# Weight transposes moved into the first aggregation of a graph network, with in-degrees of two chunks on VectorE

## The reference

```python
def _sage_layer(h, edge_src, edge_dst, deg_inv, W_self, W_neigh, b):
    msg = h[edge_src]
    agg = jax.ops.segment_sum(msg, edge_dst, num_segments=h.shape[0])
    mean = agg * deg_inv[:, None]
    return h @ W_self + mean @ W_neigh + b
# _L0_gnn_ref
deg = segment_sum(ones, edge_dst);  deg_inv = 1.0 / jnp.maximum(deg, 1.0)
h = relu(_sage_layer(x, ..., W_self0, W_neigh0, b0))
out = _sage_layer(h, ..., W_self1, W_neigh1, b1)
# _L1_gnn_ref: h = x @ W.T + b, symmetric normalisation by degree, self loops added
x = _layernorm(x + _L0_gnn_ref(x, ...))
x = _layernorm(x + _L1_gnn_ref(x, ...))
```

## Time and profile before

| | us |
|---|---|
| median of 3 runs | 849.19 |
| lowest and highest run | 848.74 and 851.98 |
| the profiled execution | 849.59 |
| its span | 847.9 |
| PE busy | 830.6 (98%) |
| DVE busy | 461.3 (54%) |
| POOL busy | 459.1 (54%) |
| ACT busy | 177.4 (21%) |
| granted TensorE clock, mean | 0.999 |

### The profile page before, as it was taken

The page is one execution under the profiler, slowest core; times in us unless marked ns, Lnnn a source line. Parts: engine busy times, 40 slices in busy tenths (PEclk is TensorE's granted clock), DMA queues, the critical chain, the costliest instruction groups (busy, mean ns, idle before and its releaser), DMA issues.

```text
span 847.9 us, 11000 instructions
## 1 busy us (share of the span) xinstructions
PE 830.6 (98%) x4295; PEld 707.9 (83%) x4295; DVE 461.3 (54%) x714; ACT 177.4 (21%) x218; POOL 459.1 (54%) x343
## 2 busy tenths in 40 slices
PE   8999999999999999999999999999999999999996
PEld 6888888888897899788888888778889889988885
DVE  6465568200017565897544677775556435455555
ACT  4111132110111113353123112222222122200000
POOL 5028887787777887885888788788620000000000
PEclk9999999999999999999999999999999999999999
DMA  9977965463776425668876668267877649555551
GB/s 332 380 304 267 350 193 168 125 176 75 213 236 180 122 57 133 249 237 286 298 282 222 243 220 284 62 176 214 240 245 255 223 150 295 189 199 199 198 193 46
DMA packets 99480, 180.52 MB, mean 213 GB/s; under 512 B 15474, under 2 KB 75898, under 8 KB 94048
## 3 DMA queue, kind: packets, MB, share of 16 engines
q1 hardware_dynamic: 60144, 124.17, 44.0%
q10 hardware_dynamic: 26896, 40.65, 13.3%
q0 software_dynamic: 12384, 14.95, 7.6%
HBM read 107.08 MB, written 72.43 MB: 212 GB/s over the span
## 4 chain that ended last, share of the span: by engine, by line
PE 61%; POOL 15%; DMA 9%; issue 8%; DVE 5%; SPq 1%; ACT 1%; POOLq 0%; ACTq 0%; DVEq 0%
PE ps L1572 19%; POOL adj_in L643 14%; PE ps L1429 12%; PE ps L1606 10%; PE ps L1589 9%; PE ps L1515 8%; DMA adj_in<-u 4%; DMA first_rows<-in_L_gnn_W_neigh 1%; DMA spare<-in_x 1%; DMA xin<-s0t_scr 1%; PE ps L1413 1%; DVE u L914 1%; PE ps L1380 1%; SPq L514 1%; DVE sacc L1303 0%
## 5 line engine op out<-in xcount | busy, mean ns | idle before, releaser
L643 POOL DMA_INDIRECT adj_out<-loops,idx_out x160 | 245.2, 1533 | 65.4 <-issue 65.4
L643 POOL DMA_INDIRECT adj_in<-mult,idx_in x160 | 198.1, 1238 | 86.8 <-issue 86.8
L1572 PE MATMUL ps<-u 128*128 128x512 f32 x840 | 190.7, 389 | 1.4 <-DVE u L914 1.4
L1572 PEld LDWEIGHTS ps<-u 128*128 128x128 f32 x840 | 157.6, 188 | 34.2 <-issue 1.6
L1484 PE MATMUL ps<-wx 128*128 128x512 f32 (+1 forms) x576 | 109.4, 351 | 1.3 <-ACT outb L761 1.3
L1484 PEld LDWEIGHTS ps<-wx 128*128 128x128 f32 x576 | 93.9, 189 | 16.9 <-ACT outb L761 1.9
L1429 PE MATMUL ps<-u 128*128 128x512 f32 x432 | 98.2, 389 | 0.0
L1515 PE MATMUL ps<-wx,u 128*128 128x256 f32 (+5 forms) x640 | 94.8, 309 | 1.2 <-DVE ht L1191 1.2
L1589 PE MATMUL ps<-u,panel_tiles 128*128 128x512 f32 (+1 forms) x400 | 93.9, 393 | 1.9 <-DVE u L914 1.9
L1429 PEld LDWEIGHTS ps<-u 128*128 128x128 f32 x432 | 81.0, 188 | 16.8
L1515 PEld LDWEIGHTS ps<-wx,u 128*128 128x128 f32 (+1 forms) x640 | 86.6, 191 | 8.2 <-DVE ht L1191 1.6
(11 more groups left out here) (167 smaller groups left out, 779.8 us busy)
## 6 DMA issues: line engine op xcount, KB each, us to landing
left_scr<-u SPq DMA_DIRECT2D x7, 2560.0 KB, 9.5
u<-left_scr SPq DMA_DIRECT2D x7, 2560.0 KB, 9.6
xt_scr<-wx ACTq DMA_DIRECT2D x10, 1024.0 KB, 9.9
u<-xt_scr SPq DMA_DIRECT2D x10, 1024.0 KB, 5.1
wx<-xt_scr SPq DMA_DIRECT2D x16, 512.0 KB, 4.0
adj_in<-u POOLq DMA_DIRECT2D x4, 1600.0 KB, 25.3
adj_out<-u POOLq DMA_DIRECT2D x4, 1600.0 KB, 16.1
wx<-adj_in SPq DMA_DIRECT2D x5, 1280.0 KB, 7.1
```

The lines of the kernel that those rows point to most:

```text
L643: pool.indirect_dma_start(table, bass.IndirectOffsetOnAxis(ap=index[0:EP, j:j + 1], axis=0), counts[0:EP, j:j + 1], None, bounds_check=CEL ...
L1572: ins = nc.tensor.matmul(ps[:, product_bank(g, i, p), :], left_op[n % 2][:, p, k, left, :], right_op[n % 2][:, k, right, :], start=(not on ...
```

## The change

- The 8 row transposes of `w_gcn` leave `mean1` and go into `mean0`, behind blocks 3, 8, 12, 14, 17, 20, 23 and 26 (`TURN_BEHIND`). There is now one slot to load into (`turn_in`) and one to copy to (`turn_out`). SP loads rows 1 to 7 ahead of its steps for blocks 7, 12, 16, 18, 21, 24 and 27 (`TURN_LOADS`); ACT copies and stores behind the ReLU of blocks 0, 5, 8, 10, 13, 16, 19 and 23 (`TURN_COPIES`).
- For chunks 0 and 1 the 10 degree matmuls are replaced: DVE sums the panel over its 10 rows of tiles (`tensor_reduce` into `sacc`), copies the sum to `colsum`, and PE makes one matmul with ones (`degrees`), behind block 0 in chunk 0 and behind block 11 (the fourth) in chunk 1. Chunks 2 and 3 keep their 10 matmuls, and now wait for the copy of a turned row, since rows are turned into the same two banks.
- The one-row matmuls for the 1/degree column and DVE's copy of it go. SP stores each chunk's row of 1/degree to memory and loads the column from there once.
- The self parts of blocks 0 to 3 are loaded during `self_turned`. The load of `b1` into `bias` comes after the blocks, because `colsum` lies in the same memory.

```diff
+    TURN_BEHIND = {3: 0, 8: 1, 12: 2, 14: 3, 17: 4, 20: 5, 23: 6, 26: 7}
+    TURN_LOADS = {7: 1, 12: 2, 16: 3, 18: 4, 21: 5, 24: 6, 27: 7}
+    TURN_COPIES = {0: 0, 5: 1, 8: 2, 10: 3, 13: 4, 16: 5, 19: 6, 23: 7}
...
+        turn_in = at("turn_in", [P, D], F32, WX_AT + 4 * (OPS + 3 * PSIZE))
+        turn_out = at("turn_out", [P, D], F32, WX_AT + 4 * (OPS + 3 * PSIZE + D))
...
-        bias = sb("bias", [P, D], F32)
+        bias = at("bias", [P, D], F32, B_AT)
+        colsum = at("colsum", [P, WIDE], F32R, B_AT)
...
+            def fetch_self(m):
+                c, d = H_BLOCKS[m]
+                for i in [S0_BLOCKS.index((b, d)) for b in {0: (0,), 1: (0, 1), 2: (1,), 3: (2,)}[c]]:
+                    sp.wait_ge(s0_stored[i % 4], 16 * (i // 4 + 1))
+                if m >= 4:
+                    sp.wait_ge(h_sum, fetch_free(m))
+                sp.dma_start(fetch_slot(m)[:, 0:CHUNKS[c][1] * T], s0t_scr[d, :, lines(CHUNKS[c])]).then_inc(s0_in[m % 8], 16)
...
+                if i == 20:
+                    sp.wait_ge(xt_turned, NT)
+                    for m in range(4):
+                        fetch_self(m)
...
+            def load_turn(k):
+                if k == 0:
+                    sp.wait_ge(s0_full, 3 * KD)
+                else:
+                    sp.wait_ge(wt_turned, k)
+                sp.dma_start(turn_in[:, :], w_gcn[k * P:(k + 1) * P, :]).then_inc(wt_in, 16)
+
+            load_turn(0)
             sp.wait_ge(m1_full[0], 16)
             load_chunk_1(1)
 
 
-            sp.wait_ge(xt_turned, NT)
             for m, (c, d) in enumerate(H_BLOCKS):
...
+                if m in TURN_LOADS:
+                    load_turn(TURN_LOADS[m])
                 if m >= 4:
-                    sp.wait_ge(h_sum, fetch_free(m))
-                sp.dma_start(fetch_slot(m)[:, 0:CHUNKS[c][1] * T], s0t_scr[d, :, lines(CHUNKS[c])]).then_inc(s0_in[m % 8], 16)
+                    fetch_self(m)
                 if m in (15, 23):
                     load_chunk_1(2 + m // 17)
+                if d == 6:
+                    t0, n = CHUNKS[c]
+                    sp.wait_ge(dinv_row_done, c + 1)
+                    sp.dma_start(dinv_scr[lines(CHUNKS[c])].rearrange("(a j) -> a j", a=1), dinv_row[0:1, c % 2, 0:n * T]
+                                 ).then_inc(dinv_stored[c % 2], 16)
...
+            for s in range(2):
+                sp.wait_ge(dinv_stored[s], 16 * 2)
+            sp.dma_start(dinv[:, :], dinv_scr.rearrange("(t p) -> p t", p=P), allow_slow_non_contiguous=True).then_inc(dinv_in, 16)
+            sp.wait_ge(deg_full, 4)
+            sp.dma_start(bias[:, :], b1.rearrange("(a d) -> a d", a=1).broadcast_to([P, D])).then_inc(bias_full, 16)
...
+            def keep_turned(k):
+                act.wait_ge(wt_turned, k + 1)
+                if k > 0:
+                    act.wait_ge(wt_stored, 16 * k)
+                nc.scalar.activation(turn_out[:, :], pair_bank(3), ACT.Copy).then_inc(wt_copied, 1)
+                act.wait_ge(wt_copied, k + 1)
+                act.dma_start(wt_scr.rearrange("(k p) o -> p k o", p=P)[:, :, k * P:(k + 1) * P],
+                              turn_out.rearrange("p (k o) -> p k o", k=KD)).then_inc(wt_stored, 16)
...
+                if m in TURN_COPIES:
+                    keep_turned(TURN_COPIES[m])
...
-                if 1 <= t <= KD:
-                    k = t - 1
-                    act.wait_ge(wt_turned, k + 1)
-                    nc.scalar.activation(late[:, k % 2, :], pair_bank(3), ACT.Copy).then_inc(wt_copied, 1)
-                    act.wait_ge(wt_copied, k + 1)
-                    act.dma_start(wt_scr.rearrange("(k p) o -> p k o", p=P)[:, :, k * P:(k + 1) * P],
-                                  late[:, k % 2, :].rearrange("p (k o) -> p k o", k=KD)).then_inc(wt_stored[k % 2], 16)
...
                 if d == 0:
+                    if c < 2:
+                        dve.wait_ge(m1_full[c], 16 * n // 2)
+                        nc.vector.tensor_reduce(sacc[:, 0:width].rearrange("p (n j) -> p n j", n=n // 2),
+                                                m1_panels[c][:, :, :, :].bitcast(F32).rearrange("p k n j -> p n j k"), AX_X, ALU.add
+                                                ).then_inc(colsum_done, 1)
+                        dve.wait_ge(colsum_done, 2 * c + 1)
+                        nc.vector.tensor_copy(colsum[:, 0:width], sacc[:, 0:width]).then_inc(colsum_done, 1)
                     dve.wait_ge(deg_full, c + 1)
                     if c >= 2:
-                        dve.wait_ge(dcol_full, c - 1)
+                        dve.wait_ge(dinv_stored[c % 2], 16)
                     nc.vector.tensor_scalar(row, ps[:, 6 + c % 2, 0:width], 1.0, None, ALU.max).then_inc(deg_read, 1)
                     dve.wait_ge(deg_read, c + 1)
                     nc.vector.reciprocal(row, row).then_inc(dinv_row_done, 1)
...
-                if d == 5:
-                    dve.wait_ge(dcol_full, c + 1)
-                    nc.vector.tensor_copy(dinv[:, t0:t0 + n], ps[:, 6 + c % 2, 0:n]).then_inc(dcol_read, 1)
...
+                        dve.wait_ge(wt_stored, 16 * KD)
...
+            dve.wait_ge(dinv_in, 16)
...
-            def turn_weights(c):
-                pe.wait_ge(wt_in[c % 2], 16 * (c // 2 + 1))
-                if c == 0:
-                    pe.wait_ge(*summed(1, 6, 2))
-                else:
-                    pe.wait_ge(wt_copied, c)
+            def turn_weights(row, c):
+                pe.wait_ge(wt_in, 16 * (row + 1))
+                pe.wait_ge(deg_read, c + 1)
+                if row > 0:
+                    pe.wait_ge(wt_copied, row)
                 for k in range(KD):
-                    ins = nc.tensor.transpose(pair_bank(3)[:, k * P:(k + 1) * P], late[:, c % 2, k * P:(k + 1) * P], ident[:, :])
+                    ins = nc.tensor.transpose(pair_bank(3)[:, k * P:(k + 1) * P], turn_in[:, k * P:(k + 1) * P], ident[:, :])
                 ins.then_inc(wt_turned, 1)
...
+            def degrees(c, width, exact):
+                pe.wait_ge(s0_free, s0_bank_free(6 + c))
+                if c == 1:
+                    pe.wait_ge(wt_copied, 2)
+                pe.wait_ge(colsum_done, 2 * c + 2)
+                bank = ps[:, 6 + c % 2, 0:width]
+                if exact:
+                    ins = nc.tensor.matmul(bank, ones_r[:, :].bitcast(F32), sacc[:, 0:width], start=True, stop=True)
+                else:
+                    ins = nc.tensor.matmul(bank, ones_r[:, :], colsum[:, 0:width], start=True, stop=True)
+                ins.then_inc(deg_full, 1)
...
-                    if c < 2:
-                        pe.wait_ge(s0_free, s0_bank_free(6 + c))
-                    else:
-                        pe.wait_ge(dcol_read, c - 1)
-                    for k in range(NT):
-                        ins = nc.tensor.matmul(ps[:, 6 + c % 2, 0:width].rearrange("p (n j) -> p n j", n=n // 2), typed(ones_r[0:rows(k), :], exact),
-                                               typed(panels[0:rows(k), k, :, :], exact), start=(k == 0), stop=(k == NT - 1))
-                    ins.then_inc(deg_full, 1)
+                    if c >= 2:
+                        pe.wait_ge(deg_read, c - 1)
+                        pe.wait_ge(wt_copied, {2: 4, 3: 7}[c])
+                        for k in range(NT):
+                            ins = nc.tensor.matmul(ps[:, 6 + c % 2, 0:width].rearrange("p (n j) -> p n j", n=n // 2),
+                                                   typed(ones_r[0:rows(k), :], exact), typed(panels[0:rows(k), k, :, :], exact),
+                                                   start=(k == 0), stop=(k == NT - 1))
+                        ins.then_inc(deg_full, 1)
                     for d in range(KD):
...
-                        if d == 2:
-                            pe.wait_ge(dinv_row_done, c + 1)
-                            for i in range(n):
-                                ins = nc.tensor.matmul(ps[:, 6 + c % 2, i:i + 1], dinv_row[0:1, c % 2, i * T:(i + 1) * T],
-                                                       ones_nt[0:1, 0:1], start=True, stop=True)
-                            ins.then_inc(dcol_full, 1)
+                        if (c, d) in ((0, 0), (1, 3)):
+                            degrees(c, width, exact)
+                        if m in TURN_BEHIND:
+                            turn_weights(TURN_BEHIND[m], 0 if m == 8 else c)
...
-                        if 1 <= t <= KD:
-                            turn_weights(t - 1)
```

More of the change, by code:

```diff
@@ L87, in build @@
         keys_scr = dram("keys_scr", [E])
+        dinv_scr = dram("dinv_scr", [PER])
         edges_scr = dram("edges_scr", [2, PAD_E], I32)
@@ L92, in build @@
         base = -(-nc.sbuf_base // 32) * 32
-        U_AT, WX_AT, R_AT, E_AT, END = (base + n for n in (0, 81920, 163840, 188416, 197120))
+        U_AT, WX_AT, R_AT, E_AT, B_AT, END = (base + n for n in (0, 81920, 163840, 188416, 197120, 201216))
         sb("arena", [P, (END - base) // 4], F32)
@@ L280, in build @@
```

(23 more changed lines are left out.)

4 lines of the change are left out of this document (removed).

## The result

| | kernel before | changed kernel |
|---|---|---|
| median us | 849.86 (848.74 to 851.98, 6 runs) | 855.61 (853.78 to 858.33, 6 runs) |
| span of the profiled execution | 847.9 | 854.8 |

The ratio is 1.0067 (95% interval 1.0048 to 1.0087): slower by 5.7 us, where 5.2 us were forecast.

The account below looks back on a forecast made before the run. PE, busy 98% of the span, was taken as the bound. -6.94 - 1.14 + 9.9 + 1.25 + 2.1 = +5.2 us gave a median of 854.4 us, range 852.5 to 856.5 (8 in 10: 850.0 to 858.0).

Parts of the forecast that it names:

- The wait for row 3: In `mean0` between blocks 14 and 15, PE waits 9.9 us for weight row 3, loaded behind chunk 2's panels.
- The clock: Behind the 9.9 us wait in `mean0`, PE runs at half rate at first: 2.1 us lost, bounds 0 and 4.2.
- the rival without this cost: The 9.9 us wait in `mean0` is there but costs no clock: 852.3 us, chance 0.17.
- Chunk 3's wait for ACT's copy: In `mean0`, chunk 3's degree matmuls wait for ACT's copy of row 6: 1.25 us, bounds 1.0 and 2.5.
- Work off PE: In `mean0`, fewer degree and column matmuls and no 1.20 us wait at block 8: -6.94 us; transposes add 6.6.
- `mean1`: 6.6 us of transposes leave `mean1`, and the 1.14 us wait for ACT's copy goes with them.
- Row 1: In `mean0`, the load of weight row 1 comes some 0 to 1 us ahead of its need.
- DVE's reduction: In `mean0`, chunk 1's sum over 5120 elements takes 5.6 us, hidden in 14 us, even at twice the time.
- beside them: In `mean0`, row 3 lands beside chunk 2's panels: wait 5.9 us, 850.4 us with the clock's loss, chance 0.12.
- "faster": Row 3 is in place when block 14 ends in `mean0`, PE never stops: -6.8 us, 842.4 us, chance 0.07.

Follow-up runs that it names:

- e3: Changed kernel with chunk 1's in-degrees again from 10 PE matmuls ahead of block 8: 848.95 us, ratio 0.9994 to the kernel before.
- e1: Changed kernel with weight row 3 loaded ahead of SP's step for block 13 instead of 16: 849.19 us, ratio 1.0000 to the kernel before.
- e9: Changed kernel with the transposes and their loads left in `mean1`: 868.74 us against 871.12 for the kernel before, ratio 0.9976.
- e4: Changed kernel with 36 throwaway matmuls filling PE's wait ahead of row 3's transposes: 853.14 us, ratio 1.0040 to the kernel before.
- e2: Changed kernel with e1's edit, and chunk 2's panels issued behind block 13's self part instead of 15's: 847.67 us, ratio 0.9974 to the kernel before.
- e11: The changed kernel run once more, unaltered: 876.49 us against 871.12 for the kernel before, ratio 1.0055.
- e5: Changed kernel with rows loaded into up to three places, row 3 and chunk 2's panels at block 13, rows 4 to 6 turned earlier: 865.77 us, ratio 0.9950.
- the repaired whole: The kernel of e5, changed kernel with loads and turns reordered; run once more: 865.85 us against 871.12 for the kernel before, ratio 0.9946.
- e12: The kernel of e8 once more, the kernel before with only the 1/degree column through memory: 865.84 us, ratio 0.9941.
- e8: Kernel before with only the 1/degree column through memory, its 20 PE matmuls gone: 866.94 us, ratio 0.9965.
- e6: Kernel before with only the self parts of blocks 0 to 3 loaded during the product ahead: 871.31 us against 870.12, ratio 1.0010.

## Why the prediction was right

The mechanism came as worked out, and most of its terms within 0.4 us. That the total comes so near, 5.7 us against 5.2, is in part luck, as the end of this list shows.

- **The wait for row 3** was the term that decided, and came as worked out: DVE's 15.6 us from the degrees to the sum of block 11 (279.98 to 295.6), SP's issue of the row 16.8 us after the degree matmul (296.61, with that matmul's successor at 279.78; forecast 16.7), 7.9 us to land (forecast 7.9), a wait of 9.99 us (forecast 9.9). e3 shows that the backlog makes it, e1 that the order hands it on, e9 that the backlog makes PE wait even without transposes.
- **The clock** cost 2.46 us (forecast 2.1, from the earlier trace rows); e4 shows that standing still is what costs it; the rival without this cost is out. The prediction's sentence from the Trainium skill (TensorE: Matmul & The Clock Gate, What's actually happening), that the idle state is the throttled one and activity releases it, agrees with this trace: 0.50 granted behind 9.99 us of idle, 0.97 in the 11 us from 309 us on.
- **Chunk 3's wait for ACT's copy**: 1.39 us (forecast 1.25). The copy waited for the store of the row before here too, if only shortly (e3 shows it long).
- **Work off PE**: without the waits and the clock, `mean0` changed by 14.8 - 9.99 - 2.46 - 1.39 - 1.41 = -0.45 us, against -6.94 + 6.56 = -0.38.
- **`mean1`** gained 9.5 us with the wait in front of it, against 7.7. Of the 1.8 us more, 1.3 are that wait, which was not forecast.
- **Row 1** was put at 0 and cost 1.41 us. It landed 11.4 us after its issue; the two blocks of weights issued in front of it took 16.4 and 13.3 us to land. That is the term that was too small. The runs show it at 0.4 (e1), 0.5 (e4) and 2.9 us (e2), and e11 has no wait for this row.
- **DVE's reduction** was taken at 5.6 us and took 9.47. It was still hidden, as the working said it would be at twice the price: the copy behind it ends at 276.1, 3.4 us ahead of the matmul that needs it.
- **The other rivals**: row 3 landed behind the panels, not beside them (1.7 us after); "faster" would have needed the sum of block 11 about 10 us sooner. e5 reaches such a state by other means, and then the kernel is in fact faster.
- **Luck in the total**: not forecast were +1.41 us for row 1, +1.1 ahead of `mean0` and +0.5 in the last stages, and on the other side -1.8 at `mean1`. They leave 1.2 us. The spans differ by 6.9 us and the medians by 5.7; that the medians lie nearer to the forecast is no merit of the working.

## What to carry to other kernels

Work taken off the bounding engine counts only if what it produced is still there in time. Moving a result behind four blocks saved 2.2 us of PE and left another engine with four blocks to catch up; follow such a backlog through the in-order queue that waits for its end, and look at each load that stands behind it. When the price of moved work is near the gain, time each part alone: the column through memory, forecast at 2.45 us, gave by itself as much as the repaired whole in e9 to e12 (5.3 us each), and 3.2 of its 4.4 us in e5 to e8. e6 has a warning too: a part tried alone must be tried where the wait that it is to remove exists.
